# Last block of a fused attention and feed-forward kernel: other engines for its square sums, its statistics and its neighbour's normalisation

## The chip, the cores and the metric

The kernel runs on one core of a Trainium2 chip. Its time is the device time in microseconds (us) of one execution. A core has engines that run their own instruction streams side by side and wait for each other through semaphores: TensorE (PE in the profile; matmuls, with its weight loads as PEld), VectorE (DVE), ScalarE (ACT), GpSimd (POOL), and SyncE (SP), which issues the DMAs here.

## The reference

The input x is 8 x 1024 tokens of 256 channels. Everything is float32.

```python
x = _layernorm(x + attention(x))          # linear attention of 16 heads, then projection Wo
def ffn(x):
    h = layer_norm(x, ln1_g, ln1_b)                       # over 256 channels
    h = h @ ternary(w1).T + b1                            # 256 -> 1024
    h = gelu(h)
    h = layer_norm(h, ln2_g, ln2_b)                       # over 1024 hidden channels
    return h @ ternary(w2).T + b2                         # 1024 -> 256
x = _layernorm(x + ffn(x))                # no gain and no bias; (x - mean) / sqrt(var + 1e-5)
```

So each token needs two variances at the end: that of its 1024 hidden values (from the mean of the values and the mean of their squares), and that of its 256 sums of residual and output.

## The kernel before, in words

The first part (up to about 280 us) is the attention of 8 batches. The second is the feed-forward part, in `NK` = 16 blocks, numbered 0 to 15, of 512 tokens; a block is `TB` = 4 tiles of 128 tokens. The change is in what is done for the last two blocks, `NK - 2` = 14 and `NK - 1` = 15, after their matmuls.

The hidden values of a block are computed in 8 chunks of 128 channels x 512 tokens (`ff_first`, L1932). ScalarE applies Gelu (L829), squares a chunk into `ff_sq` (L845) and rounds it to the high part of a split (L847); VectorE makes the low part (L1336); TensorE multiplies both parts with the second weight (`ff_second`, L1977), tokens on the partitions, into four banks of `ff_yps`, whose columns 256 and 257 collect minus the mean of the hidden values.

The mean of the squares takes a path of its own. In an ordinary block GpSimd adds the chunks 0 to 5 of `ff_sq` into `ff_accp` (`ff_square_sum`, L549, the work at L558), VectorE adds chunks 6 and 7 into `ff_accd` (L1347) and then both (L1354); TensorE transposes the sum (`ff_sum_transposes`, L1917) and VectorE reduces it (`ff_hidden_stats`, L1375) and makes the variance (L1379, L1382). In block 15 before the change GpSimd adds all eight chunks (loop at L656), and TensorE transposes `ff_accp`.

For an ordinary block the 1/sqrt is a power on GpSimd, VectorE centres the output (L1367), adds the residual (L1396), takes the statistics of the result in `ff_z` (`ff_out_stats`, L1405; aggregates at L1413), GpSimd takes the power (`ff_out_rstd`, L530 and L533), VectorE makes the shift (`ff_out_shift`, L1449) and ScalarE normalises each tile in place (`ff_normalise_out`, L862). `ff_z` has two halves: even blocks use half 0 and odd blocks half 1, so that block 15 can write its half only after block 13's store has left it (`ff_o_out`).

Block 15 is shorter. ScalarE loads its square root table (L1082), normalises block 13, scales the identity by the negative hidden means into `l_diag` (L1086), and TensorE adds the centring as four more products (L2145). ScalarE takes the square root of the hidden variance (L1088), VectorE its reciprocal (L1418). Then VectorE adds the residual out of PSUM (`last_residual`, L1426), takes statistics and aggregates per pair of tiles (L1434); ScalarE takes the square root (`last_root`, L1093), VectorE the reciprocal (L1439) and the shift (L1441); ScalarE normalises tiles 0, 1 and 2 (`last_normalise`, L1098) and VectorE tile 3 (L1677). Block 14 is normalised by ScalarE at L1089, between the hidden square root and the first `last_root`.

Each engine's order is written out by hand at the end of its own function: GpSimd L654 to L659, ScalarE L1074 to L1105, VectorE L1650 to L1678, TensorE L2122 to L2146. SyncE stores block 14 (L407) and then block 15 in two pairs of tiles (L408 to L413), in this order in one queue; it waits before each for the normalisations of what it stores.

## Time and profile before

| | us |
|---|---|
| median of 3 runs | 555.7 (555.2 to 556.03) |
| the profiled execution, its own time | 556.32 |
| its span in the profile | 554.4 |
| TensorE busy, share of the span | 535.3 (97%) |
| VectorE | 479.8 (87%) |
| ScalarE | 484.9 (87%) |
| GpSimd | 402.8 (73%) |
| mean granted TensorE clock, of full speed | 0.994 |

Busy time is the union of an engine's instructions; consecutive instructions of one engine overlap a little in the records, so a group of n can take less than n times one. The time of an execution is longer than its span, here by 1.9 us. In the rows below a time is in us from the start of the span, then comes the duration, then the engine, the line of the kernel, the operation, what it writes and reads with its shape, how many instructions of that kind stand in a row there (x4), and in brackets how long the engine was idle before it and who released it.

### The profile page before, as it was taken

The page shows a single profiled execution, that of the slowest core. Times are in us where ns is not written, and L with a number is a line of the kernel's source. Part 1 is how long each engine was busy: PE and PEld are TensorE (multiplying, and loading weights), DVE is VectorE, ACT ScalarE, POOL GpSimd, SP SyncE. Part 2 cuts the span into 40 slices and gives each one's busy share as a digit, 9 for nine tenths or more (in the row PEclk, how much of TensorE's full clock was granted, in tenths as well). Part 3 has the DMA queues.
Part 4 walks back from the last instruction along what each step waited for, and adds up shares of the span by engine and source line. Part 5 has one row for each costly group of instructions (what it writes and reads, how often), then busy time and mean ns, then how long its engine had stood idle before and what let it go on. Part 6 is the DMA issues. An engine that isn't in the chain of part 4 may idle for free.

```text
span 554.4 us, 10901 instructions
## 1 busy us (share of the span) xinstructions
PE 535.3 (97%) x3541; PEld 491.8 (89%) x3541; DVE 479.8 (87%) x1227; ACT 484.9 (87%) x964; POOL 402.8 (73%) x417
## 2 busy tenths in 40 slices
PE   8999999999999999889899999999999999999993
PEld 7999999898999989779788999899998999999992
DVE  5878998988899898958677899999999999999895
ACT  5746798798979878778889999999999999999996
POOL 2965979877797987467548877866776866776782
PEclk9999999999999999999999999999999999999997
DMA  8530060411605030142110122221022222010002
GB/s 332 210 114 1 1 228 2 167 63 59 246 1 229 1 115 39 53 165 89 76 40 17 23 77 78 78 77 50 28 77 77 77 77 68 29 61 38 39 38 115
DMA packets 12679, 46.51 MB, mean 84 GB/s; under 512 B 1360, under 2 KB 3792, under 8 KB 10448
## 3 DMA queue, kind: packets, MB, share of 16 engines
q1 hardware_dynamic: 12336, 45.28, 22.6%
q8 instruction: 29, 0.48, 0.3%
q10 hardware_dynamic: 288, 0.54, 0.3%
q14 instruction: 26, 0.21, 0.1%
HBM read 29.01 MB, written 16.81 MB: 83 GB/s over the span
## 4 chain that ended last, share of the span: by engine, by line
PE 69%; DVE 12%; ACT 11%; issue 3%; DMA 2%; POOL 2%; SPq 0%; DVEq 0%; ACTq 0%; POOLq 0%
PE ring L1973 19%; PE qps_sps_aps_then_y L1997 19%; PE qps_sps_aps_then_y L1842 8%; PE qps_sps_aps_then_y L1756 5%; PE ring L1784 5%; PE qps_sps_aps_then_y L1861 4%; DVE z L1254 4%; PE ring L1913 2%; DVE qsum L1148 2%; ACT z L786 2%; PE ring L1876 1%; PE ring L1888 1%; DVE et_lo L1113 1%; PE ring L1928 1%; DMA xc<-in_x_first_dram 1%
## 5 line engine op out<-in xcount | busy, mean ns | idle before, releaser
L1997 PE MATMUL qps_sps_aps_then_y<-ff_w_over_xc_lo,ff_a_lo_over_qw 128*128 128x258 f32 x512 | 126.2, 283 | 0.0
L1997 PE MATMUL qps_sps_aps_then_y<-ff_w_over_xc_lo,ff_a_hi_over_xc_lo 128*128 128x258 f32 x512 | 126.2, 282 | 0.0
L1336 DVE SCALAR_TENSOR_TENSOR ff_a_lo_over_qw<-ring,ff_rho,ff_a_hi_over_xc_lo 128x512 fp32r<-128x512 f32 x128 | 92.9, 744 | 15.7 <-ACT ff_a_hi_over_xc_lo L847 15.1
L1973 PE MATMUL ring<-ff_ht_hi_over_qw,t 128*128 128x512 f32 x256 | 104.2, 407 | 0.9 <-DVE ff_ht_lo_over_xc_hi L1328 0.5
L1973 PE MATMUL ring<-ff_ht_lo_over_xc_hi,t 128*128 128x512 f32 x256 | 101.2, 395 | 0.0
L1997 PEld LDWEIGHTS qps_sps_aps_then_y<-ff_w_over_xc_lo,ff_a_hi_over_xc_lo 128*128 128x128 f32 x512 | 96.8, 189 | 3.6
L1997 PEld LDWEIGHTS qps_sps_aps_then_y<-ff_w_over_xc_lo,ff_a_lo_over_qw 128*128 128x128 f32 x512 | 96.7, 189 | 3.3
L829 ACT ACTIVATE ring<-ring,bias 128x512 f32<-128x512 f32 x128 | 84.0, 685 | 7.9 <-PE ring L1973 6.9
L558 POOL TENSOR_TENSOR ff_accp_over_xt_lo<-ff_accp_over_xt_lo,ff_sq_over_ek_et_hi 128x512 f32<-128x512 f32 x66 | 86.1, 1304 | 2.9
L845 ACT ACTIVATE ff_sq_over_ek_et_hi<-ring 128x512 f32<-128x512 f32 x128 | 80.4, 628 | 0.5
L847 ACT CAST ff_a_hi_over_xc_lo<-ring 128x512 fp32r<-128x512 f32 x128 | 79.3, 620 | 0.0
L545 POOL TENSOR_TENSOR ff_x1c_over_xt_hi<-ff_x_over_w_raw_xc,ff_c_row 128x512 f32<-128x512 f32 x32 | 37.4, 1190 | 36.4 <-DVE ff_z_over_et_lo L1396 36.3
L1973 PEld LDWEIGHTS ring<-ff_ht_hi_over_qw,t 128*128 128x128 f32 x256 | 48.4, 189 | 10.4 <-issue 1.3
L1973 PEld LDWEIGHTS ring<-ff_ht_lo_over_xc_hi,t 128*128 128x128 f32 x256 | 48.2, 188 | 8.0
L460 POOL TENSOR_TENSOR qw<-qw,qinv 128x1024 f32<-128x1024 f32 x16 | 31.1, 1942 | 25.6 <-DVE qinv L1155 25.4
L1842 PE MATMUL qps_sps_aps_then_y<-r_hi,pt_hi 128*128 128x384 f32 x128 | 45.4, 355 | 2.4 <-DVE r_lo L1113 1.4
L1842 PE MATMUL qps_sps_aps_then_y<-r_lo,pt_hi 128*128 128x384 f32 x128 | 43.1, 337 | 0.0
L1842 PE MATMUL qps_sps_aps_then_y<-r_hi,pt_lo 128*128 128x384 f32 x128 | 43.0, 336 | 0.0
L1265 DVE BATCH_NORM_STATS2 bnA<-qps_sps_aps_then_y 128x6 f32<-128x256 f32 x64 | 27.2, 426 | 17.2 <-PE qps_sps_aps_then_y L1842 17.2
L439 POOL TENSOR_TENSOR xt_lo<-xt,xt_hi 128x1024 fp32r<-128x1024 f32 x16 | 38.4, 2402 | 1.3
L450 POOL TENSOR_TENSOR xt<-xt,c_row 128x1024 f32<-128x1024 f32 x16 | 38.4, 2403 | 0.7
L1756 PE MATMUL qps_sps_aps_then_y<-w_hi,xc_hi 128*128 128x256 f32 x128 | 37.2, 291 | 0.8 <-DVE qw L1138 0.6
(199 smaller groups left out, 1608.7 us busy)
## 6 DMA issues: line engine op xcount, KB each, us to landing
xt<-in_x_tok_dram SPq DMA_DIRECT2D x8, 1024.0 KB, 4.8
out_dram<-ff_z_over_et_lo SPq DMA_DIRECT2D x15, 512.0 KB, 3.2
x_scratch<-z SPq DMA_DIRECT2D x14, 514.0 KB, 3.0
ff_x_over_w_raw_xc<-x_scratch SPq DMA_DIRECT2D x14, 514.0 KB, 4.8
xc<-in_x_chan_dram SPq DMA_DIRECT2D x6, 1024.0 KB, 6.9
w_raw<-in_w_dram SPq DMA_DIRECT2D x2, 1024.0 KB, 5.3
ek<-in_x_chan_dram SPq DMA_DIRECT2D x1, 1024.0 KB, 8.2
x_scratch<-xt SPq DMA_DIRECT2D x2, 512.0 KB, 5.2
```

What stands on the lines that cost most here:

```text
L439: nc.gpsimd.tensor_tensor(xt_lo[:, ts], xt[:, b % 2, ts], xt_hi[:, ts].bitcast(F32), ALU.subtract).then_inc(xt_lo_ok, 1)
L450: nc.gpsimd.tensor_tensor(xt[:, b % 2, ts], xt[:, b % 2, ts], c_row[:].rearrange("p (o c) -> p o c", o=1).to_broadcast([P, GROUP, C]), ALU ...
L545: nc.gpsimd.tensor_tensor(ff_x1c[:, k % 2, ts], ff_x1[:, k % XB, ts, 0:C], ff_c_row[:].rearrange("p (o c) -> p o c", o=1).to_broadcast([P, ...
L558: nc.gpsimd.tensor_tensor(ff_accp[:], a, ff_sq[:, m], ALU.add).then_inc(ff_sum_p, 1)
L829: nc.scalar.activation(ff_bank(k, m), ff_bank(k, m), ACT.Gelu, bias=bias1[:, m:m + 1]).then_inc(ff_gelu_ok, 1)
L845: nc.scalar.activation(ff_sq[:, m], ff_bank(k, m), ACT.Square).then_inc(ff_sq_ok, 1)
L847: nc.scalar.copy(ff_a_hi[:, m % DEPTH], ff_bank(k, m)).then_inc(ff_hi_ok, 1)
L1336: nc.vector.scalar_tensor_tensor(out=ff_a_lo[:, m % DEPTH], in0=ff_bank(k, m), scalar=ff_rho[:, m:m + 1], in1=ff_a_hi[:, m % DEPTH].bitcas ...
L1756: last = nc.tensor.matmul(out, a, w, start=(b == 0 and h == 0 and c == 0 and k == 0), stop=(b >= 1 and c == CH - 1 and k == 2), skip_group ...
L1842: last = nc.tensor.matmul(out, l, r, start=(c == 0 and k == 0), stop=(c == CH - 1 and k == 2), skip_group_check=True)
L1973: mm = nc.tensor.matmul(ff_bank(k, m), t1[:, c, m * P:(m + 1) * P], h[:, k % 2, c], start=(c == 0 and j == 0), stop=(c == CH - 1 and j == 1))
L1997: last = nc.tensor.matmul(ff_yps[:, t, 0:C + 2], a[:, m % DEPTH, t * P:(t + 1) * P], ff_w2[:, m], start=(m == 0 and j == 0), stop=(m == FC ...
```

## The change

Semaphores `l_prev_ok`, `l_mean`, `l_sq` and small buffers `l_sum`, `l_nm`, `l_ss` are new. GpSimd adds only chunks 0 to 5 of block 15's squares and then takes its square of the mean; VectorE adds chunks 6 and 7 and the two sums; TensorE multiplies this sum with one column of ones, tile by tile, instead of transposing it, so that VectorE's reduction goes. GpSimd normalises block 14. VectorE's residuals of tiles 0 and 1 of block 15 also sum their rows, and ScalarE squares these tiles around their mean with a sum, which gives their variances; VectorE keeps the statistics of tiles 2 and 3. VectorE normalises tiles 1 and 3, ScalarE 0 and 2.

```diff
@@ SyncE
             def ff_store(k):
-                sp.wait_ge(ff_o_ok, TB * (k + 1))
+                if k == NK - 2:
+                    sp.wait_ge(l_prev_ok, TB)
+                else:
+                    sp.wait_ge(ff_o_ok, TB * (k + 1))
                 sp.dma_start(dst, ff_z[:, k % 2]).then_inc(ff_o_out[k % 2], 16)
...
             for g in range(2):
-                sp.wait_ge(l_act, g + 2)
-                if g == 1:
-                    sp.wait_ge(l_dve, 1)
+                sp.wait_ge(l_act, g + 1)
+                sp.wait_ge(l_dve, g + 1)
@@ GpSimd
             ff_out_rstd(NK - 3)
-            for m in range(5, FC):
-                ff_square_sum(NK - 1, m)
+            ff_square_sum(NK - 1, 5)
+            ff_mean_square(NK - 1)
             ff_out_rstd(NK - 2)
-            ff_mean_square(NK - 1)
+            pool.wait_ge(ff_z_rstd, NK - 1)
+            for t in range(TB):
+                nc.gpsimd.tensor_scalar(ff_z[:, NK % 2, t], ff_z[:, NK % 2, t], ff_mvZ[:, t, 0:1], ff_rsZ[:, t:t + 1],
+                                        ALU.subtract, ALU.mult).then_inc(l_prev_ok, 1)
@@ ScalarE
             for t in range(TB):
+                if t == TB - 1:
+                    act.wait_ge(ff_r_eps, NK)
+                    nc.scalar.activation(l_root[:, 0], ff_var[:], ACT.Sqrt).then_inc(l_hidden_root, 1)
                 nc.scalar.activation(l_diag[:, t], ident[:], ACT.Copy, scale=ff_nmu[:, t:t + 1]).then_inc(l_diag_ok, 1)
-            act.wait_ge(ff_r_eps, NK)
-            nc.scalar.activation(l_root[:, 0], ff_var[:], ACT.Sqrt).then_inc(l_hidden_root, 1)
-            ff_normalise_out(NK - 2, (0, 1, 2, 3))
-            def last_root(g):
-                act.wait_ge(ff_z_var, TB * (NK - 1) + 2 * g + 2)
-                nc.scalar.activation(l_root[:, 1, 2 * g:2 * g + 2], l_mv[:, 2 * g:2 * g + 2, 1], ACT.Sqrt, bias=eps[:, 0:1]
-                                     ).then_inc(l_root_ok, 1)
+            def last_squares():
+                act.wait_ge(l_mean, 1)
+                for t in range(2):
+                    nc.scalar.activation(ff_xn[:, t], ff_z[:, (NK - 1) % 2, t], ACT.Square, bias=l_nm[:, t:t + 1],
+                                         accum_out=l_ss[:, t:t + 1]).then_inc(l_sq, 1)
...
-            last_root(0)
+            last_squares()
+            act.wait_ge(l_sq, 2)
+            nc.scalar.activation(l_root[:, 1, 0:2], l_ss[:], ACT.Sqrt, bias=eps[:, 0:1], scale=1.0 / C).then_inc(l_root_ok, 1)
             last_normalise(0)
-            last_normalise(1)
-            last_root(1)
+            act.wait_ge(ff_z_var, TB * (NK - 1) + 2)
+            nc.scalar.activation(l_root[:, 1, 2:4], l_mv[:, 2:4, 1], ACT.Sqrt, bias=eps[:, 0:1]).then_inc(l_root_ok, 1)
             last_normalise(2)
@@ VectorE
+            def last_hidden_variance():
+                dve.wait_ge(ff_r_tr, NK)
+                dve.wait_ge(ff_r_sq, NK)
+                nc.vector.scalar_tensor_tensor(out=ff_var[:], in0=ff_sum_bank(NK - 1)[:, 0:TB], scalar=1.0 / F,
+                                               in1=ff_msq[:], op0=ALU.mult, op1=ALU.subtract).then_inc(ff_r_var, 1)
+                dve.wait_ge(ff_r_var, NK)
+                nc.vector.tensor_scalar(ff_var[:], ff_var[:], 0.0, EPS, ALU.max, ALU.add).then_inc(ff_r_eps, 1)
+            def last_residual(t):        # as before, and for t < 2 with accum_out=l_sum[:, t:t + 1]
...
+            def last_means():
+                dve.wait_ge(ff_z_ok, TB * (NK - 1) + 2)
+                nc.vector.tensor_scalar(l_nm[:], l_sum[:], -1.0 / C, None, ALU.mult).then_inc(l_mean, 1)
...
             ff_act_low(NK - 1, 7)
-            ff_out_stats(NK - 2, (0, 1))
+            ff_square_sum(NK - 1, 7)
+            ff_square_total(NK - 1)
+            ff_out_stats(NK - 2, (0,))
+            ff_hidden_mean(NK - 1)
+            ff_out_stats(NK - 2, (1,))
+            last_hidden_variance()
             ff_out_stats(NK - 2, (2, 3))
             ff_out_variance(NK - 2)
-            ff_hidden_mean(NK - 1)
-            ff_hidden_stats(NK - 1)
-            ff_out_shift(NK - 2)
             last_hidden_inverse()
-            last_residual((0, 1))
-            ff_out_stats(NK - 1, (0, 1))
-            last_variance(0)
-            last_residual((2, 3))
-            last_shift(0)
+            last_residual(0)
+            last_residual(1)
+            last_means()
+            last_residual(2)
+            last_residual(3)
             ff_out_stats(NK - 1, (2, 3))
-            last_variance(1)
-            last_shift(1)
-            dve.wait_ge(l_nmr, 2)
-            nc.vector.tensor_scalar(... tile 3 ...)
+            last_inverse(0)
+            nc.vector.tensor_tensor(l_shift[:, 0:2], l_nm[:], l_rs[:, 0:2], ALU.mult).then_inc(l_nmr, 1)
+            dve.wait_ge(ff_z_stat, TB * NK - 2)
+            nc.vector.memset(fence[:], 0.0)
+            for t in (2, 3):
+                nc.vector.bn_aggr(l_mv[:, t], ff_bnZ[:, t]).then_inc(ff_z_var, 1)
+            last_normalise(1)
+            last_inverse(1)
+            nc.vector.scalar_tensor_tensor(out=l_shift[:, 2:4], in0=l_mv[:, 2:4, 0], scalar=-1.0, in1=l_rs[:, 2:4],
+                                           op0=ALU.mult, op1=ALU.mult).then_inc(l_nmr, 1)
+            last_normalise(3)
@@ TensorE
-                else:                                             # ff_sum_transposes of block 15
-                    pe.wait_ge(ff_sum_p, P_ADDS * k + FC - 1)
-                    ff_bank_free(k, 5)
+            def last_square_sums():                               # called after the loop over the blocks
+                pe.wait_ge(ff_sum_d, D_ADDS * NK)
+                ff_bank_free(NK - 1, 5)
+                for t in range(TB):
+                    last = nc.tensor.matmul(ff_sum_bank(NK - 1)[:, t:t + 1], ff_accd[:, t * P:(t + 1) * P], ones[:, 0:1],
+                                            start=(t == 0), stop=(t == TB - 1), skip_group_check=True)
+                last.then_inc(ff_r_tr, 1)
```

## Rows read from the trace of the kernel before

**Rows 1.** stretches; us, busy us (instructions) per engine, TensorE clock, DMA share, GB/s
```profile
545.00:555.00 10.00, 0.96 (x5) 0.50 (x3) 5.08 (x24) 4.34 (x10) 0.00 (x0) 0.67 0.33 129
```

**Rows 2.** chain of waits, its end; start us, us, what
```profile
541.51 1.98 ACT ff_z_over_et_lo L862 x4
...
543.51 2.65 DMA out_dram<-ff_z_over_et_lo
...
550.88 0.60 ACT ff_z_over_et_lo L1098
```

**Rows 3.** VectorE's timeline before the gate (start us, us, instruction), and one line's durations
```profile
541.27 1.39 DVE L1405 BATCH_NORM_STATS2 ff_bnZ<-ff_z_over_et_lo 128x6 f32<-128x256 f32 x4
...
543.02 0.17 DVE L1360 TENSOR_REDUCE ff_nmu<-qps_sps_aps_then_y 128x4 f32<-128x8 f32 x1
544.34 0.69 DVE L1375 TENSOR_REDUCE ff_sums<-ring 128x4 f32<-128x512 f32 x1 [1.15 <-PE ring L1928]
...
545.70 0.18 DVE L1418 RECIPROCAL ff_rsH<-l_root 128x4 f32<-128x4 f32 x1 [0.19 <-ACT l_root L1088]
...
L1354 DVE TENSOR_TENSOR ff_accd_over_xt_lo<-ff_accd_over_xt_lo,ff_accp_over_xt_lo x15: 694/694/694, 297.7 to 526.6; 128x512 f32<-128x512 f32 x15
```

**Rows 4.** VectorE's timeline from the first residual of block 15
```profile
546.24 0.88 DVE L1426 SCALAR_TENSOR_TENSOR ff_z_over_et_lo<-qps_sps_aps_then_y,ff_rsH,ff_x1c_over_xt_hi 128x256 f32<-128x256 f32 x2 [0.37 <-DMA out_dram<-ff_z_over_et_lo]
...
549.05 0.74 DVE L1405 BATCH_NORM_STATS2 ff_bnZ<-ff_z_over_et_lo 128x6 f32<-128x256 f32 x2
...
549.93 0.15 DVE L1434 BATCH_NORM_AGGREGATE l_mv<-ff_bnZ 128x2 f32<-128x6 f32 x1
550.48 0.17 DVE L1439 RECIPROCAL l_rs<-l_root 128x2 f32<-128x2 f32 x1 [0.40 <-ACT l_root L1093]
550.68 0.16 DVE L1441 SCALAR_TENSOR_TENSOR l_shift<-l_mv,l_rs 128x2 f32<-128x2 f32 x1
```

**Rows 5.** ScalarE's timeline, from its table load on
```profile
540.01 1.28 ACT L1082 ACT_TABLE_LOAD   x1
...
543.39 1.26 ACT L1086 ACTIVATE zjunk<-ident,ff_nmu 128x128 f32<-128x128 f32 x4
...
549.17 1.09 ACT L1098 ACTIVATE ff_z_over_et_lo<-ff_z_over_et_lo,l_shift,l_rs 128x256 f32<-128x256 f32 x2 [0.78 <-DVE l_shift L1441]
550.17 0.28 ACT L1093 ACTIVATE l_root<-l_mv,eps 128x2 f32<-128x2 f32 x1
```

**Rows 6.** TensorE's timeline: products with one column, and block 15's last matmul
```profile
67.62 0.50 PE L1699 MATMUL qps_sps_aps_then_y<-wabs,ones 128*128 128x1 f32 x4
...
542.71 0.28 PE L1997 MATMUL qps_sps_aps_then_y<-ff_w_over_xc_lo,ff_a_lo_over_qw 128*128 128x258 f32 x1
```

**Rows 7.** GpSimd's timeline at the end
```profile
539.20 4.32 POOL L558 TENSOR_TENSOR ff_accp_over_xt_lo<-ff_accp_over_xt_lo,ff_sq_over_ek_et_hi 128x512 f32<-128x512 f32 x3
...
543.76 1.02 POOL L533 TENSOR_TENSOR ff_rsZ<-ff_veZ,nhalf 128x4 f32<-128x4 f32 x1
```

**Rows 8.** timeline, residuals and squares that sum their rows, first stage
```profile
288.18 0.21 ACT L778 ACTIVATION_READ_ACCUMULATOR zjunk<-xt,znm 128x1 f32 x1
288.27 0.52 ACT L778 ACTIVATE zjunk<-xt,znm 128x256 f32<-128x256 f32 x1
288.67 0.21 ACT L778 ACTIVATION_READ_ACCUMULATOR zjunk<-xt,znm 128x1 f32 x1
...
289.19 0.48 DVE L1254 SCALAR_TENSOR_TENSOR xt<-xt,rsA 128x256 f32<-128x256 f32 x1
...
289.72 0.17 DVE L1259 TENSOR_SCALAR znm<-zsum 128x4 f32<-128x4 f32 x1
```

**Rows 9.** VectorE's timeline, one row; then durations of two lines (min/median/max ns)
```profile
540.10 0.59 DVE L1449 SCALAR_TENSOR_TENSOR ff_nmr<-ff_mvZ,ff_rsZ 128x4 f32<-128x4 f32 x1
...
L497 POOL TENSOR_SCALAR w_raw<-w_raw,wscale x8: 696/722/1320, 78.5 to 198.5; 128x512 f32<-128x512 f32 x8
...
L1321 DVE TENSOR_SCALAR ff_xn<-ff_x_over_w_raw_xc,ff_rs x64: 336/348/354, 251.8 to 502.6; 128x256 f32<-128x256 f32 x64
```

More of the change, by code:

```diff
@@ L158, in both_halves @@
         l_root = sb("l_root", [P, 2, TB])
+        l_sum, l_nm, l_ss = sb("l_sum", [P, 2]), sb("l_nm", [P, 2]), sb("l_ss", [P, 2])
         tern_bias = sb("tern_bias", [P, 3])
@@ L248, in both_halves @@
             sem(s) for s in ("z_ok", "z_mean", "z_sq", "z_var", "z_eps", "z_rstd", "z_fin", "x1_ok"))
+        l_prev_ok, l_mean, l_sq = sem("l_prev_ok"), sem("l_mean"), sem("l_sq")
         l_diag_ok, l_centred, l_hidden_root, l_hidden_inv, l_root_ok = (
@@ L1418, in last_hidden_inverse @@
                 nc.vector.reciprocal(ff_rsH[:], l_root[:, 0]).then_inc(l_hidden_inv, 1)
-            def last_residual(ts):
-                dve.wait_ge(l_hidden_inv, 1)
-                wait_for(dve, ff_o_out[(NK - 1) % 2], 16 * ((NK - 1) // 2))
-                for t in ts:
-                    dve.wait_ge(l_centred, t + 1)
-                    dve.wait_ge(ff_x1c_ok, PIECES * (NK - 1) + t * PIECES // TB + 1)
-                    nc.vector.scalar_tensor_tensor(
-                        out=ff_z[:, (NK - 1) % 2, t], in0=ff_yps[:, t, 0:C], scalar=ff_rsH[:, t:t + 1],
-                        in1=ff_x1c[:, (NK - 1) % 2, t], op0=ALU.mult, op1=ALU.add).then_inc(ff_z_ok, 1)
@@ L1430, in last_variance @@
-            def last_variance(g):
-                dve.wait_ge(ff_z_stat, TB * (NK - 1) + 2 * g + 2)
-                nc.vector.memset(fence[:], 0.0)
-                for n in range(2 * g, 2 * g + 2):
-                    nc.vector.bn_aggr(l_mv[:, n], ff_bnZ[:, n]).then_inc(ff_z_var, 1)
-            def last_shift(g):
+            def last_hidden_variance():
[5 more added lines that the diff above has]
+                nc.vector.tensor_scalar(ff_var[:], ff_var[:], 0.0, EPS, ALU.max, ALU.add).then_inc(ff_r_eps, 1)
@@ new lines, in last_residual @@
+            def last_residual(t):
+                if t == 0:
+                    dve.wait_ge(l_hidden_inv, 1)
+                    wait_for(dve, ff_o_out[(NK - 1) % 2], 16 * ((NK - 1) // 2))
+                dve.wait_ge(l_centred, t + 1)
+                dve.wait_ge(ff_x1c_ok, PIECES * (NK - 1) + t * PIECES // TB + 1)
+                total = {"accum_out": l_sum[:, t:t + 1]} if t < 2 else {}
+                nc.vector.scalar_tensor_tensor(
+                    out=ff_z[:, (NK - 1) % 2, t], in0=ff_yps[:, t, 0:C], scalar=ff_rsH[:, t:t + 1],
+                    in1=ff_x1c[:, (NK - 1) % 2, t], op0=ALU.mult, op1=ALU.add, **total).then_inc(ff_z_ok, 1)
@@ L1440, in last_shift, with last_normalise @@
                 dve.wait_ge(l_rstd, g + 1)
-                nc.vector.scalar_tensor_tensor(out=l_shift[:, ts], in0=l_mv[:, ts, 0], scalar=-1.0, in1=l_rs[:, ts],
-                                               op0=ALU.mult, op1=ALU.mult).then_inc(l_nmr, 1)
+            def last_normalise(t):
+                dve.wait_ge(l_nmr, t // 2 + 1)
+                nc.vector.tensor_scalar(ff_z[:, (NK - 1) % 2, t], ff_z[:, (NK - 1) % 2, t], l_rs[:, t:t + 1],
+                                        l_shift[:, t:t + 1], ALU.mult, ALU.add).then_inc(l_dve, 1)
             def ff_out_shift(k):
@@ L1917, in ff_sum_transposes @@
             def ff_sum_transposes(k):
-                if not 0 <= k < NK:
+                if not 0 <= k < NK - 1:
                     return
-                if k < NK - 1:
-                    pe.wait_ge(ff_sum_d, D_ADDS * (k + 1))
-                    ff_bank_free(k + 1, 1)
-                else:
-                    pe.wait_ge(ff_sum_p, P_ADDS * k + FC - 1)
-                    ff_bank_free(k, 5)
-                acc = ff_accd if k < NK - 1 else ff_accp
+                pe.wait_ge(ff_sum_d, D_ADDS * (k + 1))
+                ff_bank_free(k + 1, 1)
                 for t in range(TB):
-                    last = nc.tensor.transpose(ff_sum_bank(k)[:, t * P:(t + 1) * P], acc[:, t * P:(t + 1) * P],
+                    last = nc.tensor.transpose(ff_sum_bank(k)[:, t * P:(t + 1) * P], ff_accd[:, t * P:(t + 1) * P],
                                                ident[:])
+                last.then_inc(ff_r_tr, 1)
[5 more added lines that the diff above has]
+                                            start=(t == 0), stop=(t == TB - 1), skip_group_check=True)
                 last.then_inc(ff_r_tr, 1)
@@ L2141, in _ @@
                 ff_second(k, 7)
+            last_square_sums()
             for t in range(TB):
```

3 lines of the change are left out of this document (1 added, 2 removed).

## The prediction

> **What bounds the kernel now.** I read the stretches by engine first, then the chain of waits backwards from the last instruction, then each engine's own timeline from 540 us on. Blocks are counted 0 to 15; the change touches blocks 14 and 15 and nothing that runs before 541 us, where TensorE is the busiest engine (97% of the whole span). After 545 us it is different: in the last 10 us of the span TensorE is busy 0.96 us, VectorE 5.08 and ScalarE 4.34 [rows 1]. So the end is a chain of short instructions that hand over to each other, and only its order counts.
>
> The chain shows its links [rows 2]: ScalarE normalises the four tiles of block 13 until 543.49, their store starts at 543.51 and lands at 546.16, and the last instruction, ScalarE's normalisation of tile 2 of block 15, ends at 551.48. VectorE's first residual of block 15 starts at 546.24 after waiting 0.37 us for this store [rows 4], because blocks 13 and 15 share one half of `ff_z`. What ended last there is the store: the reciprocal of the hidden deviation was done at 545.88 [rows 3]. I call 546.24 the gate. From the gate to the end of the last instruction it is 5.24 us, and from there to the end of the span another 2.92 us, the last store and its wait.
>
> **Part 1, the square sums (before the gate).** Removed: two of GpSimd's three additions, which run 4.32 us from 539.20 [rows 7], 1.44 each; TensorE's transposes waited for the last of them, and so VectorE's reduction of 128x512 waited 1.15 us and then took 0.69 [rows 3]. Added on VectorE: an addition of chunks 6 and 7 and one of its sum with GpSimd's, 0.69 us each by the row of the second kind [rows 3]. They start at 541.27, in the place of the first statistics, and end at 541.27 + 0.69 + 0.04 + 0.69 = 542.69. GpSimd's chunk 5 is done by 539.20 + 1.44 = 540.64, so nothing waits for it. On TensorE the four products with a ones column come behind the last matmul of the second layer (start 542.71) and are eight passes in f32; four such passes with one column took 0.50 [rows 6], so eight take 1.0 to 1.1, from 542.83 to 543.93. The hidden mean stays where it is, at 543.02, since it waits for those same matmuls to end at 542.99 [rows 3, 6]. Then two small instructions for the variance, 0.20 each as in the reciprocal-to-shift step [rows 4]: 543.97 to 544.37. VectorE goes on with the last two statistics of block 14 (0.74 for two [rows 4]) from 544.29 to 545.03, the aggregates (0.36 from the end of the statistics at 542.66 to the next start at 543.02 [rows 3]), and the reciprocal of the hidden deviation, which ends at 545.6. The square root for it fits on ScalarE between the third and fourth diagonal copy, which start at 543.39 and take 0.32 each [rows 5], so at 544.4. The correction products follow on TensorE and end near 545.6, before tile 2 or 3 is asked for.
>
> So the reciprocal comes about 0.3 us earlier than before, and it is worth nothing: the store of block 13 still lands at 546.16, since the table load at 540.01 [rows 5] and the four normalisations ahead of it are as they were. The cover is 546.24 - 545.6 = 0.6 us; if the eight passes cost twice their row (+1.1), the gate would move by 0.5. A gain from this part is excluded, because the store alone holds the gate.
>
> **Part 2, block 14's normalisation goes to GpSimd.** ScalarE loses four instructions, about 2 us by the same four of block 13 [rows 2], which lay beside VectorE's residuals and statistics. By itself it gives nothing, but it frees ScalarE for part 3. On GpSimd: aggregates of block 14 end at 545.5, the addition of epsilon takes 0.2 to 0.3, the power 1.02 [rows 7], so the four tensor_scalar instructions start at about 546.9. Nothing in the trace shows this instruction on 128x256 with two pointers. The nearest row is GpSimd's tensor_scalar on 128x512, 0.696 at best and 0.722 in the median [rows 9]; half the columns give 0.45 with some 0.2 fixed, and the upper bound is an addition of two 128x512 operands, 1.44 [rows 7]. I take 0.45, the same kind of instruction: the four end at 548.7, the store of block 14 is issued then and lands at 548.7 + 2.65 = 551.4 [rows 2]. Before, it was issued when ScalarE's four were done, about 2 us after the root ahead of the reciprocal at 545.70 [rows 3], so near 547.6. SyncE now waits 1 us longer in front of the two last stores, but the first of them isn't ready before 549.8. Nothing is lost.
>
> **Part 3, from the gate.** VectorE's two residuals step by 0.40 (0.88 for two [rows 4]); they now sum their rows as well. A residual with such a sum is in the trace: the instruction for the means started 0.53 after the start of the last residual, 289.19 to 289.72, and took 0.17 [rows 8]. So residuals at 546.24 and 546.64, means at 547.17 to 547.34. On ScalarE a square with its sum: start to end of the accumulator read is 288.27 to 288.88, 0.61, and the next one starts 0.49 later, the step between the two reads at 288.18 and 288.67 [rows 8]. Hence squares at 547.38 and 547.87, the second sum at 548.48, the square root of two variances (0.28 [rows 5]) from 548.52 to 548.80. Removed from VectorE are two statistics, a fence and two aggregates ahead of that root. VectorE in the meantime: residuals of tiles 2 and 3 at 547.28 and 547.68, their statistics from 548.08 to 548.82. It is free just when the root is done. Reciprocal at 548.84, shift at 549.04 to 549.20 [rows 4]. ScalarE normalises tile 0 at 549.24 and can take the next instruction 0.50 later, as it did between 549.17 and 550.17, two tiles [rows 5]; so the second root starts at 549.74. Its aggregates are ready earlier: 0.29 us after the shift is issued (statistics end at 549.79, aggregates at 550.08 [rows 4]), near 549.4. Tile 1 goes to VectorE beside ScalarE.
>
> That is the whole gain. Before, two normalisations stood in front of the second root on ScalarE, so it started at 550.17 though the variances were there at 550.08; the last instruction ended 551.48 - 550.17 = 1.31 after it [rows 2, 5]. The same tail, root, reciprocal, shift, one normalisation, now starts at 549.74 and ends at 551.05. Gain 0.43 us. The profiled execution took 556.32 us with a span of 554.4; it would take 555.89 with 553.97. The shown runs have a median of 555.7, 0.6 below that execution, so the forecast is 555.7 - 0.43 = 555.3.
>
> **Where a rule speaks against it.** VectorE and GpSimd disturb each other. The tiny shift instruction at 540.10, two SBUF operands, took 0.59 where the same kind takes 0.16, and ended when GpSimd's addition did, at 540.64 [rows 4, 9]. In the tail the residuals read one operand from PSUM, so they are not of that kind. The shifts are, but they come at 549.04, after GpSimd's 548.7. The means at 547.17 are a tensor_scalar with one SBUF operand and fall among GpSimd's four; the trace has 64 larger ones of this kind, 336 to 354 ns [rows 9], but none beside a long GpSimd instruction. The Trainium skill, "VectorE: DVE Perf Modes", section "Mode 2×_2P — use both read ports for one tensor", says that an fp32 tensor_scalar out of SBUF uses both read ports, and "GPSIMD Engine Reference", section "1. Specifications", that such an instruction contends with GpSimd as well. By that rule the means can wait for a GpSimd instruction to end; no run here shows it yet.
>
> **The rivals.**
> (a) The means wait for one GpSimd normalisation, up to 0.45 us by its estimate. It is all on the path (means, squares, root), and it eats the gain: 555.7, no change. For it: the stall of the tiny shift. Against it: that one had two operands. The rule named above would make it so.
> (b) GpSimd's normalisations are slow, at the upper bound. Slower than before: 4 x 1.3 to 1.44 from 546.9 ends at 552.1 to 552.7, and all three last stores queue behind the wait for it on SyncE. Block 14's store lands 2.65 later, 554.8 at best, and 256 KB more behind it, up to half of that again; a landing lies 0.3 ahead of the span's end (551.48 + 2.65 against 554.4), so the span ends 0.7 to 2.0 later than before. I take 1.4: 557.1. It decides from 0.95 us per instruction on, when GpSimd's end passes 550.7. For it: one tensor_scalar on 128x512 took 1.320 [rows 9]. Against it: the other seven.
> (c) The square on ScalarE needs a table that the square root's doesn't have, so loads of 1.28 us [rows 5] come in front of the square and of the root. The first can hide in ScalarE's idle time before 547.38, the second can't: +1.28 to +2.56 - 0.43, so 556.5 to 557.8. Against it: the whole trace has three loads, and squares run among the exponentials and among the Gelus without one.
> (d) The variance of the hidden layer is late by more than its cover of 0.6, by the ones products or by the wait for GpSimd's square of the mean. The gate moves by up to 0.5: 555.4 to 555.8.
> (e) More than 1.1 us is gained. It would need the gate to move forward, and nothing ahead of the store of block 13 changes. 554.5 or less.
>
> **How the numbers follow.** Forecast (555.0 to 555.6) 0.64, (a) 0.15, (d) 0.08, (b) 0.06, (c) 0.03, (e) 0.04. The measurement tells 0.2%, 1.1 us, from no change. The forecast, (a) and (d) lie within that: 0.87. Slower by more than that are (c) and most of (b), 0.08; faster (e) and a little of the forecast, 0.05. The three runs shown spread over 0.8 us. The range starts 0.7 below the forecast, for that spread and a tail in which VectorE's means come sooner, and reaches to 556.2, over (a) and (d): 554.6 to 556.2.
>
> **What would show it.** In the trace of the changed kernel: the first residual of block 15 still waits for the store of block 13 and starts at 546.2; the hidden reciprocal ends before 545.9; each GpSimd normalisation takes 0.4 to 0.5 and the last ends before 549; the means take 0.17 and not 0.6; no table load after 541.3; the second root of block 15 starts 3.5 us after the first residual (before: 3.93); the last instruction ends 4.8 us after it (before: 5.24). The prediction is wrong if the first residual waits for ScalarE or VectorE instead of the store, if a store waits for GpSimd after 551, or if the second root starts no earlier than before.

## The result, and the profile after

Each comparison below is of runs on the same chip: medians, and a ratio to the kernel before with its 95% interval, which can differ from the quotient of the medians by up to 0.0008. Runs 1 to 4, 5 to 8 and 9 to 11 each share their runs of the kernel before. One execution of the kernel before among those of runs 5 to 8 took 751.39 us at a granted clock of 0.655 and is left out of the medians and ratios.

| | before | after |
|---|---|---|
| time, us | 555.79 (555.04 to 556.68, 8 runs) | 557.47 (556.7 to 557.72, 8 runs) |
| ratio to before | | 1.0029 [1.002, 1.0039] |
| profiled execution, its own time, us | 556.32 | 556.7 |
| its span, us | 554.4 | 554.9 |

The change made the kernel slower by 1.7 us, 0.29%. The forecast was 555.3, a little faster, and 557.47 lies outside its range, 554.6 to 556.2. It is the mechanism of rival (b), which had 6 in 100.

The chain of waits of the kernel after ends on another engine than before, where it ended with ScalarE's L1098 [rows 2]. Its last rows (start us, us, what; `issue` is time in which the engine waited for nothing that the profile shows, POOLq is GpSimd's own sequencer):

```profile
543.77 1.02 POOL ff_rsZ L537
544.79 0.05 issue
544.84 1.28 POOLq L88
546.12 3.62 POOL ff_z_over_et_lo L665 x3
```

The last thing that anyone waited for is GpSimd's normalisation of block 14. One line's instructions (count, minimum/median/maximum in ns), and then what SyncE's queue waited for from 530 us on (us in total, times, the longest):

```profile
L665 POOL TENSOR_SCALAR ff_z_over_et_lo<-ff_z_over_et_lo,ff_mvZ,ff_rsZ x4: 1218/1222/1225, 544.9 to 548.5; 128x256 f32<-128x256 f32 x4
```

```profile
SPq L380 <- POOL ff_z_over_et_lo L665: 7.8, 1, 7.8
SPq L419 <- DMA out_dram<-ff_z_over_et_lo: 3.0, 1, 3.0
```

Each instruction takes 1.22 us where I took 0.45, and the four last until 549.74. SyncE sits in front of block 14's store all that time. The three last stores, 512, 256 and 256 KB, are then issued one behind the other, at 549.77, 550.20 and 550.67; before, block 14's was issued at 547.7. The last row is the final wait of the queue, 3.0 us where the kernel before had 2.1.

VectorE's timeline from its sum of squares on, then ScalarE's from the squares, and TensorE's products with the ones column:

```profile
540.14 0.69 DVE L1364 TENSOR_TENSOR ff_accd_over_xt_lo<-ff_accd_over_xt_lo,ff_accp_over_xt_lo 128x512 f32<-128x512 f32 x1
...
541.98 0.16 DVE L1433 SCALAR_TENSOR_TENSOR ff_var<-ring,ff_msq 128x4 f32<-128x4 f32 x1 [0.20 <-PE ring L1959]
...
543.33 0.14 DVE L1428 RECIPROCAL ff_rsH<-l_root 128x4 f32<-128x4 f32 x1
544.32 0.48 DVE L1445 SCALAR_TENSOR_TENSOR ff_z_over_et_lo<-qps_sps_aps_then_y,ff_rsH,ff_x1c_over_xt_hi 128x256 f32<-128x256 f32 x1 [0.85 <-DVE ff_rsH L1428]
...
545.25 0.21 DVE L1451 TENSOR_SCALAR l_nm<-l_sum 128x2 f32<-128x2 f32 x1
...
547.41 0.60 DVE L1461 TENSOR_SCALAR ff_z_over_et_lo<-ff_z_over_et_lo,l_rs,l_shift 128x256 f32<-128x256 f32 x1
...
548.58 0.64 DVE L1461 TENSOR_SCALAR ff_z_over_et_lo<-ff_z_over_et_lo,l_rs,l_shift 128x256 f32<-128x256 f32 x1
```

```profile
545.50 0.51 ACT L1101 ACTIVATE ff_xn<-ff_z_over_et_lo,l_nm 128x256 f32<-128x256 f32 x1 [2.63 <-DVE l_nm L1451]
...
547.87 0.28 ACT L1114 ACTIVATE l_root<-l_mv,eps 128x2 f32<-128x2 f32 x1
548.57 0.60 ACT L1106 ACTIVATE ff_z_over_et_lo<-ff_z_over_et_lo,l_shift,l_rs 128x256 f32<-128x256 f32 x1 [0.43 <-DVE l_shift L1704]
```

```profile
540.95 0.99 PE L1959 MATMUL ring<-ones,ff_accd_over_xt_lo 128*128 128x1 f32 x8
```

The gate, the start of block 15's first residual, is at 544.32. The bracket blames VectorE's own reciprocal, but that ended at 543.47, 0.85 earlier; what came then is the landing of block 13's store, issued at 541.64, which took 2.6 us. When a named releaser was long done, look for a DMA. The compute after the gate did what was planned: the second root starts 3.55 us after the gate (before 3.93) and the last compute instruction of ScalarE and VectorE ends 4.90 after it (before 5.24 [rows 2, 4]). But the span ends 10.58 us after the gate, where before it was 8.16. So the last block costs 2.4 us more, and the kernel only 1.7: the rest came back in a place that the change was not meant to touch (experiments 5 and 6).

In the following table "block 14's store" (its issue), "to last compute" (of ScalarE and VectorE) and "to end" are measured from the first residual of block 15 in the profiled execution; spans are printed to 0.1 us, so a difference under 0.1 in "to end" says nothing. "Block" is the step between two stores of the feed-forward part (L375 before: 335.49 to 483.69 for nine blocks, 148.20/9 = 16.47), and "last wait" is SyncE's at the very end.

| kernel | GpSimd, one tile | block 14's store | to last compute | to end | last wait | block | ratio to before |
|---|---|---|---|---|---|---|---|
| before | - | 1.42 | 5.24 | 8.16 | 2.1 | 16.47 | 1 |
| after | 1.22 | 5.45 | 4.90 | 10.58 | 3.0 | 16.38 | 1.0029 [1.002, 1.0039] |
| 2: GpSimd multiplies only | 0.46 | 2.42 | 4.79 | 7.72 | 2.1 | 16.38 | 0.9976 [0.9965, 0.9986] |
| 3: GpSimd starts earlier | 1.21 | 3.61 | 4.90 | 8.73 | 3.0 | 16.38 | 0.9997 [0.9988, 1.0006] |
| 4: other order, two tiles | 1.21 | 1.55 | 4.80 | 8.05 | 2.5 | 16.37 | 0.9979 [0.9971, 0.9988] |
| 5: before, buffers moved 96 B | - | 1.48 | 5.23 | 8.23 | 2.1 | 16.38 | 0.9983 [0.9975, 0.9992] |
| 6: after, buffers not moved | 1.21 | 5.42 | 4.87 | 10.50 | 3.0 | 16.47 | 1.0034 [1.0022, 1.0047] |
| 7: product and sum | 0.54 | 3.09 | 4.92 | 8.25 | 2.5 | 16.38 | 0.9979 [0.997, 0.9988] |
| 8: 4 and 7 together | 0.55 | 1.17 | 4.87 | 8.23 | 2.5 | 16.38 | 0.9978 [0.9968, 0.9987] |
| 9: before, moved 32 B | - | 1.40 | 5.23 | 8.16 | 2.1 | 16.49 | 1.0015 [1.0005, 1.0024] |
| 10: before, moved 64 B | - | 1.46 | 5.23 | 8.23 | 2.1 | 16.46 | 1.0008 [1.0, 1.0017] |
| 11: 7, buffers not moved | 0.54 | 3.06 | 4.88 | 8.19 | 2.5 | 16.47 | 0.9999 [0.999, 1.0008] |

### The profile page after: what moved, and what is told of

The parts are those of the page before. It is cut to its first block, busy times and chain, and to the rows that moved or that the text cites. A ratio compares the mean times of both kernels' runs of the same rounds, so it can differ in the third digit from the quotient of the medians.

```text
span 554.9 us, 10908 instructions
## 1 busy us (share of the span) xinstructions
PE 535.1 (96%) x3545; PEld 492.8 (89%) x3545; DVE 481.2 (87%) x1226; ACT 483.6 (87%) x963; POOL 405.5 (73%) x419
## 4 chain that ended last, share of the span: by engine, by line
PE 72%; DVE 12%; ACT 8%; issue 3%; POOL 3%; DMA 1%; POOLq 0%; DVEq 0%; ACTq 0%
PE qps_sps_aps_then_y L2028 19%; PE ring L2004 19%; PE qps_sps_aps_then_y L1870 7%; PE qps_sps_aps_then_y L1784 7%; PE ring L1812 6%; PE qps_sps_aps_then_y L1889 4%; DVE z L1264 3%; PE ring L1941 2%; PE ring L1904 2%; PE ring L1916 1%; DVE qsum L1158 1%; DVE et_lo L1123 1%; PE ring L1951 1%; ACT zjunk L785 1%; POOL ff_accp_over_xt_lo L562 1%
## 5 line engine op out<-in xcount | busy, mean ns | idle before, releaser
L562 POOL TENSOR_TENSOR ff_accp_over_xt_lo<-ff_accp_over_xt_lo,ff_sq_over_ek_et_hi 128x512 f32<-128x512 f32 x64 | 83.6, 1306 | 2.6
```

The costliest lines, as they stand in the source:

```text
L562: nc.gpsimd.tensor_tensor(ff_accp[:], a, ff_sq[:, m], ALU.add).then_inc(ff_sum_p, 1)
```

## The experiments

**1. What GpSimd's instruction costs by itself.** Extra instructions behind all the work of the kernel before, on GpSimd alone and then beside VectorE; its own time means nothing.

```
g = nc.gpsimd.tensor_scalar                   # seven of its lines; L670 and L676 to L678 are left out here
g(out, s, mean, rs, ALU.subtract, ALU.mult)   # L668, as in the change; L672 with 512 columns
g(out, s, rs, 0.0, ALU.mult, ALU.add)         # L669; L673 with 512 columns
g(out, s, rs, mean, ALU.mult, ALU.add)        # L671
g(out, s, mean, 2.0, ALU.subtract, ALU.mult)  # L674
g(out, s, rs, None, ALU.mult)                 # L675
# then VectorE's kinds of the last block, during eight of the first (L1703 on) and alone (L1714 on)
```

> The kernel before with a row of extra instructions behind its last store's data: first GpSimd alone with eleven forms of tensor_scalar and tensor_tensor, then eight of its two-pointer normalisations beside nine of VectorE's tail instructions, then the same nine alone. Theory: the second pointer operand makes the instruction slow, so the two-pointer forms take 1.22 us on 128x256 with nothing beside them, and the forms with one pointer or none about 0.45. Rival 1: the instruction is 0.45 by itself and was slow in the changed kernel only because VectorE ran beside it; then all forms take about 0.45 alone, and 1.2 in the second stage. Rival 2: any normalisation of 256 columns costs 1.2 and the 0.70 of the first stage's 128x512 was the exception; then all forms take 1.2. For VectorE: 0.41 for its two-pointer tensor_scalar alone and 0.60 or more beside GpSimd, if it needs what GpSimd holds; the residual out of PSUM (0.48) and the statistics (0.41) the same in both stages. The time of the whole kernel says nothing here.

GpSimd's timeline, and VectorE's beside it and alone:

```profile
550.54 1.22 POOL L668 TENSOR_SCALAR ff_sq_over_ek_et_hi<-ff_sq_over_ek_et_hi,ff_mvZ,ff_rsZ 128x256 f32<-128x256 f32 x1 [6.60 <-ACT ff_z_over_et_lo L1120]
551.74 0.48 POOL L669 TENSOR_SCALAR ff_sq_over_ek_et_hi<-ff_sq_over_ek_et_hi,ff_rsZ 128x256 f32<-128x256 f32 x1
...
552.58 0.56 POOL L671 TENSOR_SCALAR ff_sq_over_ek_et_hi<-ff_sq_over_ek_et_hi,ff_rsZ,ff_mvZ 128x256 f32<-128x256 f32 x1
553.12 2.07 POOL L672 TENSOR_SCALAR ff_sq_over_ek_et_hi<-ff_sq_over_ek_et_hi,ff_mvZ,ff_rsZ 128x512 f32<-128x512 f32 x1
555.17 0.69 POOL L673 TENSOR_SCALAR ff_sq_over_ek_et_hi<-ff_sq_over_ek_et_hi,ff_rsZ 128x512 f32<-128x512 f32 x1
555.84 1.14 POOL L674 TENSOR_SCALAR ff_sq_over_ek_et_hi<-ff_sq_over_ek_et_hi,ff_mvZ 128x256 f32<-128x256 f32 x1
556.95 0.94 POOL L675 TENSOR_SCALAR ff_sq_over_ek_et_hi<-ff_sq_over_ek_et_hi,ff_rsZ 128x256 f32<-128x256 f32 x1
```

```profile
560.41 0.64 DVE L1703 TENSOR_SCALAR ff_yc_over_xt_lo<-ff_x1c_over_xt_hi,l_rs,l_shift 128x256 f32<-128x256 f32 x1 [10.17 <-POOL ff_sq_over_ek_et_hi L678]
...
562.20 0.47 DVE L1706 SCALAR_TENSOR_TENSOR ff_yc_over_xt_lo<-qps_sps_aps_then_y,l_rs,ff_x1c_over_xt_hi 128x256 f32<-128x256 f32 x1
...
563.65 0.39 DVE L1710 TENSOR_SCALAR l_ve<-l_rs 128x2 f32<-128x2 f32 x1
563.71 0.33 DVE L1711 TENSOR_TENSOR l_ve<-l_rs 128x2 f32<-128x2 f32 x1
570.07 0.41 DVE L1714 TENSOR_SCALAR ff_yc_over_xt_lo<-ff_x1c_over_xt_hi,l_rs,l_shift 128x256 f32<-128x256 f32 x1 [6.03 <-POOL ff_x_over_w_raw_xc L680]
```

Alone, with nobody beside it, the instruction of the change takes 1.22: no contention makes it slow. A theory of mine, that the second pointer is what costs, falls: with two pointers but a product and a sum it takes 0.56, and with one pointer but a difference and a product 1.14. The pair of operations decides. By the two widths the slow pair costs (2.07 - 1.22)/256 = 3.3 ns a column and the fast one (0.69 - 0.48)/256 = 0.8. The row that I had halved, 0.722 for 128x512 at L497 [rows 9], is of the fast kind; that its operations were a product and a sum (ALU.mult, ALU.add) stood in the code, and I didn't ask.

**2. A fast instruction in the same place.** The mean's subtraction is left out, so this only prices the time.

```diff
-ff_mvZ[:, t, 0:1], ff_rsZ[:, t:t + 1], ALU.subtract, ALU.mult
+ff_rsZ[:, t:t + 1], 0.0, ALU.mult, ALU.add
```

> The changed kernel, but GpSimd only multiplies block 14 by its 1/sqrt, one pointer and an immediate; the subtraction of the mean is left out. Theory: the slow two-pointer instruction is the whole loss. At 0.45 each GpSimd ends before 549 in the time of the profile before, no store waits for it, and the time is 0.4 us under the kernel before, 555.4, ratio 0.999. Rival: the loss lies in the new order of the square sums or in the stores, then it stays near 557.4, ratio 1.003.

```profile
545.53 1.84 POOL L665 TENSOR_SCALAR ff_z_over_et_lo<-ff_z_over_et_lo,ff_rsZ 128x256 f32<-128x256 f32 x4
```

554.36 against 555.61. Four in 1.84 us, and everything else of the change as it was: the end comes 2.86 us earlier after the gate than in the kernel after. This one instruction is the whole loss. Block 14's store is issued at 547.40, 2.42 us after the gate, almost where the prediction had it (548.7 - 546.24 = 2.46), and the tail is 0.44 shorter than before (7.72 against 8.16), as planned.

**3. The slow instruction, started earlier.** GpSimd adds all eight chunks again, the head of the last block is as before, and block 14's statistics come first, so that its normalisation starts at 543.02.

```diff
-            ff_square_sum(NK - 1, 5)
+            for m in range(5, FC):
+                ff_square_sum(NK - 1, m)
 # VectorE: ff_out_stats(NK - 2, (0, 1)) right behind ff_act_low(NK - 1, 7); TensorE transposes ff_accp
```

> The changed kernel with the square sums of block 15 as before (GpSimd adds all chunks, transposes, reduction) and the statistics of block 14 ahead of them again; GpSimd still normalises block 14 at 1.22 each. Theory: the head part is what starts GpSimd late: its 1/sqrt of block 14 is ready 1.9 us earlier against the first residual, the four normalisations end about 3.7 us after the gate instead of 5.4, ahead of the last tiles (4.9), and the kernel is 0.3 us faster than before: 555.5, ratio 0.9995. Rival: the 4.9 us of GpSimd cost the same wherever they start, because VectorE is stalled by them: ratio 1.002 or more.

```profile
543.02 4.83 POOL L666 TENSOR_SCALAR ff_z_over_et_lo<-ff_z_over_et_lo,ff_mvZ,ff_rsZ 128x256 f32<-128x256 f32 x4
```

555.36 against 555.61, no difference (and that with moved buffers, which runs 5 and 6 price). GpSimd's four take as long as in the kernel after, but they end 3.6 us after the gate instead of 5.4. Block 14's store is issued at 547.88, the compute ends at 549.17, and the last wait of SyncE is still 3.0: the stores meet. Between the kernel after, this one and run 2 the end moves with block 14's store (5.45, 3.61 and 2.42 after the gate; 10.58, 8.73 and 7.72 to the end), while GpSimd's busy time is the same in two of them. The gate itself, at 544.27, follows the reciprocal here, which with the old head ended at 544.24.

**4. Another order: block 13 first, two tiles of block 14 for each engine.** ScalarE normalises block 13 before its table load, GpSimd takes tiles 2 and 3 of block 14 and ScalarE 0 and 1.

```diff
+            ff_normalise_out(NK - 3, (0, 1, 2, 3))
             (table load)
-            ff_normalise_out(NK - 3, (0, 1, 2, 3))
+            ff_normalise_out(NK - 2, (0, 1))          # behind the diagonal copies
-            for t in range(TB):                       # GpSimd
+            for t in (2, 3):
```

> A version of my own: the new statistics and the ones products (on GpSimd's full sum), block 13's normalisation ahead of the square root's table load, and block 14's tiles 0 and 1 normalised by ScalarE and 2 and 3 by GpSimd. Theory: the gate is the store of block 13, which is issued 0.7 us earlier; the gate then comes 0.6 to 0.7 earlier, the tail takes 4.8 instead of 5.24, and GpSimd's two instructions are done before: 1.1 us faster than before, 554.7, ratio 0.998. Rival: the table load now stands in front of the diagonals and the hidden root, and the gate moves to the reciprocal or to the centring products: 555.3, ratio 0.9992.

```profile
545.45 0.48 DVE L1449 SCALAR_TENSOR_TENSOR ff_z_over_et_lo<-qps_sps_aps_then_y,ff_rsH,ff_x1c_over_xt_hi 128x256 f32<-128x256 f32 x1 [0.33 <-DMA out_dram<-ff_z_over_et_lo]
```

554.45 against 555.61: faster than both kernels, though GpSimd's instruction is the slow one (how much of it is the moved buffers stands under runs 5 and 6). Two of them end at 546.98, soon enough. The gate is still set by block 13's store, issued at 542.33 and landed 3.02 later.

**5 and 6. Where the blocks became shorter.** In the kernel after, nine blocks take 147.42 us (334.70 to 482.12), in the one before 148.20, though no instruction of them was changed. Three small buffers were added in front of many others, among them large ones. Run 5 is the kernel before with these three, unused; run 6 is the kernel after with their contents inside two buffers that lie idle by then.

```diff
+        l_sum, l_nm, l_ss = sb("l_sum", [P, 2]), sb("l_nm", [P, 2]), sb("l_ss", [P, 2])     # 5, and nothing else
-        l_sum, l_nm, l_ss = sb("l_sum", [P, 2]), sb("l_nm", [P, 2]), sb("l_ss", [P, 2])     # 6
+        l_sum, l_nm, l_ss = l_ve[:, 0:2], l_ve[:, 2:4], ff_sums[:, 0:2]
```

> The kernel before with the three small buffers of the change allocated in the same place and used by nothing, so every buffer behind them lies 24 bytes further. Theory: the changed kernel's blocks are shorter (16.38 us each against 16.47 in the profiles, the 512-column matmuls 403 and 392 ns against 406 and 395) because of these addresses alone. Then this kernel has the short blocks and is 1.2 us faster than before, ratio 0.998. Rival: the short blocks come from the instructions that the change moved, or from chance between builds; then ratio 1.000 and 16.47 per block.

> The changed kernel with its sums, means and square sums kept in buffers that were already there, so that no address moves. Theory: the change itself costs what the tail shows, 2.4 us from the first residual of block 15 to the end, and its addresses give 1.2 back; without the shift it is 2.4 to 2.8 us slower than before, ratio 1.0045 to 1.005, blocks of 16.47 us. Rival: the addresses don't matter, ratio 1.003 as measured for the changed kernel.

Groups of the first layer's products between 335 and 483 us (count, busy us, mean ns), run 5 and then run 6:

```profile
L1974 PE MATMUL ring<-ff_ht_hi_over_qw,t 128*128 128x512 f32 x145 | 58.4, 403 | 0.0
L1974 PE MATMUL ring<-ff_ht_lo_over_xc_hi,t 128*128 128x512 f32 x145 | 56.9, 392 | 0.0
```

```profile
L2004 PE MATMUL ring<-ff_ht_hi_over_qw,t 128*128 128x512 f32 x145 | 58.9, 406 | 0.0
L2004 PE MATMUL ring<-ff_ht_lo_over_xc_hi,t 128*128 128x512 f32 x144 | 56.9, 395 | 0.0
```

Run 5: 555.12 against 555.78, and 16.38 us a block. Run 6: 558.08 against 555.78, and 16.47 a block. Unused buffers make the kernel before 0.7 to 0.9 us faster (by the medians and by the ratio; the interval is 0.4 to 1.4, and 1.2 was expected). The product durations and the block step follow the addresses in both directions. The time of run 6 alone doesn't tell 1.0044, the full loss of the tail, from the 1.0029 of the kernel after; its interval holds both, and its 1.0034 is below the 1.0045 to 1.005 that was expected.

Runs 2, 4, 7 and 8 carry the moved buffers too. Of their 0.9976 to 0.9979 run 5 has 0.9983 by the buffers alone, so what they gain by themselves, 0.0004 to 0.0007, is inside the intervals; of these four only run 7 was also made with the buffers in their old places (run 11). (A buffer takes a multiple of 32 bytes here, so three of 8 bytes move the rest by 96 bytes per partition, not by the 24 that the expectations say.)

**7. The change with GpSimd's fast pair.** GpSimd makes the shift, minus the mean over the deviation, with two tiny instructions and then multiplies and adds.

```diff
+            nc.gpsimd.tensor_tensor(ff_nmr[:], ff_nmr[:], ff_rsZ[:], ALU.mult).then_inc(l_pn, 1)   # ff_nmr: minus the mean
-ff_mvZ[:, t, 0:1], ff_rsZ[:, t:t + 1], ALU.subtract, ALU.mult
+ff_rsZ[:, t:t + 1], ff_nmr[:, t:t + 1], ALU.mult, ALU.add
```

> The changed kernel with GpSimd normalising block 14 as a multiplication and an addition (it makes the shift itself, two small instructions more) instead of a subtraction and a multiplication. Theory: the operations decide, not the second pointer; 0.56 each as measured alone, the store of block 14 leaves before the last tiles are ready, the tail is 4.8 us and nothing queues. With the addresses as in the changed kernel 1.2 + 0.4 = 1.6 us faster than before: 554.1, ratio 0.997; 3.3 us faster than the changed kernel. Rival (second pointer): 1.2 each and 557.4.

```profile
545.85 2.17 POOL L674 TENSOR_SCALAR ff_z_over_et_lo<-ff_z_over_et_lo,ff_rsZ,ff_nmr 128x256 f32<-128x256 f32 x4
```

555.06 against 555.78. The same computation as the change in 0.54 us a tile, and faster than both kernels, but not by the 1.6 us that was expected: its ratio is that of the moved buffers within the noise. The shift's two instructions start the four tiles 0.90 us after the gate (0.55 in run 2) and each tile takes 0.08 more, so block 14's store goes out 3.09 after the gate and the tail is 8.25, as long as before. The last compute ends 0.13 later than in run 2, by as much as VectorE's shift L1706 takes longer beside GpSimd (0.29 where L1697 took 0.16).

**8. Runs 4 and 7 together.**

```diff
-            for t in range(TB):                       # GpSimd, with ALU.subtract, ALU.mult
+            for t in (2, 3):                          # with ff_rsZ, ff_nmr and ALU.mult, ALU.add; the rest as in run 4
```

> The version with block 13's normalisation ahead of the table load, with GpSimd's two tiles as a multiplication and an addition. Theory: block 14's store is issued 0.7 us earlier (546.3 against 547.0 beside a gate of 545.4) and is out of the last stores' way, 0.2 to 0.3 us less: ratio 0.9974. Rival: the last stores don't meet it anyway, ratio 0.998 as without the edit.

554.74 against 555.78; its ratio is that of run 4 and of run 7, so the rival holds. With two tiles the slow pair was fast enough already; GpSimd even waits 0.79 us for VectorE's shift (L1473). The gate, at 544.77, follows the reciprocal now, and no longer the store. Its compute ends 0.37 us sooner than before after the gate, yet the span doesn't (8.23): SyncE's last wait is 2.5, as in run 4, although the transfers don't touch there. In both the last pair of tiles takes 2.8 us from issue to landing, where it took 2.5 before and 2.4 in run 2. Why is open.

**9 and 10. Which property of the addresses.** One and two unused buffers in the kernel before, 32 and 64 bytes.

> The kernel before with one unused buffer in front of the later ones. A buffer takes a multiple of 32 bytes, so this moves every later one by 32 bytes per partition; the three small buffers of the change (and of the run before with three) moved them by 96, not by the 24 that their contents take. Theory (what counts is on which of the two 32-byte halves of 64 bytes a buffer begins, and 96 and 32 are alike in that): blocks of 16.38 us, first-layer products of 403 and 392 ns, time 0.9983 of before. Rival (the distance itself counts, or the order of the buffers): blocks of 16.47 us or something between, time 0.999 to 1.0.

> The kernel before with two unused buffers, a shift of 64 bytes. Theory of the 32-byte halves: nothing changes, blocks of 16.47 us, products of 406 and 395 ns, time 1.000 of before. Rival (any shift away from the addresses of before gains): 16.38 us and 0.9983.

First-layer products as above, run 9 and then run 10:

```profile
L1974 PE MATMUL ring<-ff_ht_hi_over_qw,t 128*128 128x512 f32 x144 | 58.4, 406 | 0.0
L1974 PE MATMUL ring<-ff_ht_lo_over_xc_hi,t 128*128 128x512 f32 x144 | 56.9, 395 | 0.0
```

```profile
L1974 PE MATMUL ring<-ff_ht_hi_over_qw,t 128*128 128x512 f32 x144 | 58.4, 405 | 0.0
L1974 PE MATMUL ring<-ff_ht_lo_over_xc_hi,t 128*128 128x512 f32 x145 | 57.2, 394 | 0.0
```

556.43 and 556.13 against 555.60. The theory of the halves falls by run 9: 32 bytes don't gain although they share their half of 64 with 96. That any move gains falls by both. Run 9 is a little slower than before, and its block step, 16.49, explains only 0.3 us of the 0.8; run 10 can't be told from no change (its interval starts at 1.0). That addresses matter to 0.1 or 0.2% is shown; by which rule stays open. No kernel with 96 bytes ran on the chip of runs 9 to 11. The unmoved kernels of two chips, 6 and 11, both have blocks of 16.47, so nothing points at the chip.

**11. What the change is worth without the moved buffers.** Run 7 with the buffers of run 6.

> The change with GpSimd's normalisation as product and sum, and the three small buffers inside others, so that nothing is shifted. Theory (the fast pair of operations brings the planned gain of the tail of 0.4 us, and the shift was the rest): blocks of 16.47 us, GpSimd's four in 2.2 us, 0.9993 of before. Rival (what the tail gains up to the last instruction is lost between it and the end of the span, where the last stores meet): 1.000, and the span ends 8.2 us after the first residual, as before.

555.76 against 555.60, ratio 0.9999 [0.999, 1.0008]. The last compute ends 4.88 after the gate, 0.36 earlier than before, and the span ends 8.19 after it, as before. Transfers from 549 to 556 us in 40 slices (busy share in tenths), of the kernel before, of run 11 and of run 2:

```profile
DMA  9999200000008999100899810000000000001000
```

```profile
DMA  0089999997999999873000000000000010000000
```

```profile
DMA  9998998106999300000000000010000000000000
```

Before, block 14's transfer was over when the first pair of tiles was stored (at 550.29), and there is a gap between the two pairs. In run 11 block 14's store is issued when GpSimd's last tile is done, 3.06 us after the gate; before it was issued 1.4 after the gate. So the three transfers touch, the two pairs take 3.2 and 2.8 us from issue to landing instead of 2.5 each, and SyncE's last wait is 2.5 instead of 2.1. That is where the 0.4 us of the tail goes. In run 2 block 14's store went out 0.64 earlier after the gate; it still touched the first pair, but the last pair was clear of it, the last wait was 2.1 and the gain stayed. That touching is the only cause isn't shown, since in runs 4 and 8 the last pair takes 2.8 and the last wait is 2.5 as well, without it. The interval also holds 0.9993, so by the time alone the gain isn't excluded; by the profile it is gone in this execution.

## Why the prediction was wrong

**What bounds the end.** Right. The gate is block 13's store, before and after, and in run 4 as well (in runs 3 and 8 the reciprocal comes last).

**Part 1.** Right. The eight products with the ones column took 0.99 (1.0 to 1.1 was said), the reciprocal was done 0.85 before the gate (0.6 was said), and it gained nothing: from the last of the nine blocks' stores to the gate it is 62.20 us in the kernel after and 62.21 in run 3 with the old head.

**Part 2, the step that failed: "I take 0.45, the same kind of instruction".** It measured 1.22, and the decision point given for rival (b), 0.95, was passed. The sum made for (b), four of 1.3 to 1.44, three stores behind the wait, 557.1, came within 0.4 us of the result, but in part by luck. It took 1.4 for the tail, which lost 2.4, and the moved buffers, which it didn't have, gave 0.7 to 0.9 back. What it had too small is the stores: it counts 256 KB behind block 14's store, but both pairs follow, 512 KB, and from the end of GpSimd's last tile to the end of the span it took 5.16 us, where (b)'s terms give 3.0 to 4.3. (Its own terms at the dear end, 552.7 + 2.65 + 1.3 + 0.3, also give 2.6 later than before and not 2.0.) And 0.95 is too dear a point: with the four starting at 546.9 as predicted, the store position of run 11, 3.06 after the gate, where nothing is gained, is reached at 0.6 per tile (an estimate, (549.30 - 546.9)/4). The error was in the choice between the ends: "the nearest row" was nearest by its name and not by what it computes. With ends of 0.45 and 1.44 and the decision at 0.95, in the middle between them, the dear side deserved far more than 0.06.

**"Nothing is lost", block 14's store a little later.** At the place where the prediction had it this was right: in run 2 the store goes out 2.42 after the gate (2.46 was said), and the planned 0.44 is gained. The reason given, that the next store isn't ready before 549.8, is not enough. In run 11 block 14's store also goes out before the next one is ready (548.57 and 549.21), only 0.6 us later than the prediction had it, and the gain is gone. So the plan hung on 0.45 for a reason that the prediction didn't see, and with the same result computed as product and sum it needs two small instructions more and misses that place.

**Part 3.** Right in its working: second root 3.55 after the gate (3.5), last compute 4.90 (4.8), root, reciprocal and shift as said, no table load. Of rival (a) there is only 0.04: the means took 0.21 and not 0.17. But VectorE's two normalisations took 0.60 and 0.64 instead of 0.41, the contention that the prediction looked for at the wrong instruction; they start with ScalarE's of 0.60, so it cost next to nothing (the last ends 0.05 after ScalarE's).

**What it did not have at all.** That new buffers move old ones. It gave back 0.7 to 0.9 us (run 5) of the 2.4 lost in the tail, which leaves 1.5 to 1.7; 1.7 was measured. The statement that the change touches nothing before 541 us was true of the instructions and not of their operands' addresses.

## What to carry to other kernels

Price an instruction by its own pair of operations, not by its name; where the trace has no such row and the price decides the sign, spread the chances over the interval. Before normalising on GpSimd, write it as product and sum, and count the instructions that make the shift. Where a kernel ends in stores, count when each of the last ones is issued and how long its transfer lasts: compute that ends earlier gained nothing here once the last transfer had to follow the others directly. And when a change adds a buffer, try the old kernel with that buffer alone first.

## What the runs showed of the hardware that was not expected

- GpSimd's tensor_scalar on 128x256 f32 takes 0.48 to 0.56 for product and sum with a pointer, 0.94 for a single product, 1.14 to 1.22 for difference and product (run 1).
- While GpSimd runs such an instruction, VectorE's tensor_scalar on 128x256 takes 0.64 to 0.75 instead of 0.41, and on 128x2 a tensor_scalar takes 0.39 and a tensor_tensor 0.33 instead of 0.15 (run 1); the residual out of PSUM (0.47) and the statistics (0.41) keep their times, and GpSimd isn't slowed (9.68 for eight). The Trainium skill, "SBUF — State Buffer", section "Who interferes with whom", says that a tensor_scalar in its two-port mode and an instruction with two SBUF inputs share a pair of ports with GpSimd, and that one with at most one SBUF input outside that mode doesn't. By that rule, the trace agrees. The same section says that the one that comes second waits for the whole instruction of the other. That the trace doesn't show: VectorE's first tensor_scalar ran from 560.41 to 561.05 and ended before GpSimd's first, 560.35 to 561.58, did.
- Moving the later buffers by 96 bytes shortened 128x512 products from 406 and 395 to 403 and 392 ns (run 5); moved by 32 bytes they took 406 and 395, by 64 bytes 405 and 394 (runs 9 and 10).
